# First cross attention of a decoder: one turn per loop body, written pairs of banks, weighed sums evicted by VectorE

## The reference

```python
NUM_HEADS, HEAD_DIM = 16, 16
SCALE = HEAD_DIM ** (-0.5)
Q = (x @ Wq.T).reshape(B, xN, NUM_HEADS, HEAD_DIM)
KV = (z @ Wkv.T).reshape(B, zN, 2, NUM_HEADS, HEAD_DIM)
K, V = KV[:, :, 0], KV[:, :, 1]
attn = jnp.einsum('bqhd,bkhd->bhqk', Q, K) * SCALE
attn = jax.nn.softmax(attn, axis=-1)
O = jnp.einsum('bhqk,bkhd->bqhd', attn, V).reshape(B, xN, DIM)
return O @ Wo.T
```

## Time and profile before

| What | Value |
|---|---|
| runs of the kernel, us | 3433.4, 3438.81, 3424.18; median 3433.4 |
| the profiled execution | 3433.98 us, its span 3432.2 us |
| mean granted TensorE clock | 0.972 |
| PE busy over the span | 3200.4 us (93%) |
| PEld / DVE / ACT / POOL busy | 2364.1 / 1767.5 / 1515.0 / 866.3 us |
| instructions recorded | 77662 |
| the changed stage, turn 0 to the start of turn 15 | 641.70 to 1169.72 us of the span |
| row maxima, L1779 | 256, mean 906 ns |
| exponents, L1726 | 256, mean 668 ns |
| packets of the queues of kind "instruction" | q8 123 with 2.02 MB, q14 29 with 0.24 MB |

### The profile page before, as it was taken

The page is one execution under the profiler, slowest core; times in us unless marked ns, Lnnn a source line. Parts: engine busy times, 40 slices in busy tenths (PEclk is TensorE's granted clock), DMA queues, the critical chain, the costliest instruction groups (busy, mean ns, idle before and its releaser), DMA issues. The chain is left out here.

```text
span 3432.2 us, 77662 instructions
## 1 busy us (share of the span) xinstructions
PE 3200.4 (93%) x26274; PEld 2364.1 (69%) x26275; DVE 1767.5 (51%) x4684; ACT 1515.0 (44%) x4278; POOL 866.3 (25%) x982
## 2 busy tenths in 40 slices
PE   8999999898988899999998999999999999999982
PEld 6777776455555566677776776777777777767871
DVE  4555555555555555222223654666666666663433
ACT  4555555344444421222222326666666666642220
POOL 1000000211111100233332110132323323346773
PEclk9999999899999999999999999999999999999996
DMA  8500000300000041211113000010000000025774
GB/s 276 164 0 0 0 0 0 145 13 11 14 13 13 30 147 51 66 32 30 30 26 79 17 0 5 25 40 19 17 13 11 14 13 12 25 75 151 210 207 133
DMA packets 136484, 182.54 MB, mean 53 GB/s; under 512 B 36156, under 2 KB 108601, under 8 KB 135308
## 3 DMA queue, kind: packets, MB, share of 16 engines
q1 hardware_dynamic: 84112, 133.96, 12.6%
q0 software_dynamic: 45760, 26.67, 4.8%
q10 hardware_dynamic: 6460, 19.66, 1.6%
HBM read 116.11 MB, written 103.61 MB: 64 GB/s over the span
## 5 line engine op out<-in xcount | busy, mean ns | idle before, releaser
L1309 DVE TENSOR_REDUCE e_nmx<-PS 128x1 f32<-128x361 f32 x416 | 221.3, 532 | 340.8 <-PE PS L1156 334.9
L931 POOL DMA_INDIRECT slot_rows<-r_row,r_rows_now x256 | 256.6, 1002 | 336.8 <-DVE e_p L1316 290.2
L1779 DVE TENSOR_REDUCE b_nmx<-PS 100x2 f32<-100x722 f32 x256 | 224.9, 906 | 216.8 <-PE PS L1571 216.8
L1156 PE MATMUL PS<-e_cT,e_qT 128*128 128x361 f32 x832 | 333.4, 483 | 0.0
L2709 PE MATMUL PS<-c_wgu,c_tile_xT 128*128 x912 | 290.7, 462 | 7.4 <-issue 6.6
L1261 ACT ACTIVATE e_pT<-PS 121x384 f32<-121x384 f32 (+1 forms) x416 | 199.0, 479 | 220.6 <-PE PS L1163 220.5
L1163 PEld LDWEIGHTS PS<-ident,e_p 128*121 128x121 f32 x1248 | 198.0, 184 | 96.2 <-ACT e_pT L1261 0.4
L1266 ACT ACTIVATE e_p<-PS,e_nmx 128x361 f32<-128x361 f32 x416 | 232.4, 559 | 36.2 <-DVE e_nmx L1309 36.2
L2709 PEld LDWEIGHTS PS<-c_wgu,c_tile_xT 128*128 128x128 f32 x912 | 169.8, 191 | 84.2 <-issue 9.4
L1156 PEld LDWEIGHTS PS<-e_cT,e_qT 128*128 128x128 f32 x832 | 145.9, 190 | 115.0 <-issue 108.6
L2973 POOL DMA_INDIRECT sum<-f_y,f_y_token x128 | 199.5, 1559 | 73.8 <-issue 46.9
(11 more groups left out here) (345 smaller groups left out, 6556.6 us busy)
## 6 DMA issues: line engine op xcount, KB each, us to landing
f_w<-in_f_W SPq DMA_DIRECT2D x64, 384.0 KB, 3.8
slot_rows<-a_empty SPq DMA_DIRECT2D x1, 21504.0 KB, 65.3
f_xg<-slot_rows SPq DMA_DIRECT2D x64, 336.0 KB, 4.0
c_wgu<-in_c_GU ACTq DMA_DIRECT2D x8, 1408.0 KB, 6.9
sum<-X SPq DMA_DIRECT2D x2, 3200.0 KB, 58.2
f_sums<-sum SPq DMA_DIRECT2D x16, 400.0 KB
b_cT<-in_ctx_T SPq DMA_DIRECT2D x32, 181.5 KB, 2.4
e_cT<-in_ctx_T SPq DMA_DIRECT2D x32, 181.5 KB, 2.3
```

What stands on the lines that cost most here:

```text
L931: pool.indirect_dma_start(out=self.rows, in_=self.row[:, u, :], in_offset=None, out_offset=bass.IndirectOffsetOnAxis(ap=self.rows_now[:, u ...
L1156: sr.fill_done(pe.matmul(sr.at(f"s{m}", ROWS, CTX), qT[:, at:at + ROWS], cT[:, u, 0:CTX], start=True, stop=True), f"s{m}")
L1309: dve.tensor_reduce(nmx[:, m:m + 1], sr.at(f"s{m}", ROWS, CTX), AX.X, ALU.max, negate=True).then_inc(max_ready, 1)
L1779: sr.move_done(dve.tensor_reduce(nmx[:, g // PAR % 2, 2 * half:2 * half + 2, 16 * (1 - r)], sr.both(f"s{g}{half}", S, CTX), AX.X, ALU.max, ...
```

## The change

It has three parts.

1. `qT` has one buffer. Before ScalarE overwrites it (in slot 1), VectorE copies the part that the shift of slot 2 still needs (the last tile of element 1) to a new tile `kept`, at the end of slot 0's shift; ScalarE waits for that on a new semaphore `queries_kept`. With one buffer the `par` argument goes away everywhere, and the loop body holds one turn: 15 passes, turns 0 to 14, and turn 15 written out.
2. `Pairs.plan` takes the pair of each name as a list. Slots 0 to 6 have the same pairs as before; in slot 7 the names take 1, 2, 1, 2 (7, 8, 7, 8 modulo 3) instead of 1, 2, 0, 1.
3. `move_sums` moves from ScalarE to VectorE. It stands at the end of a slot, ahead of the next slot's row maxima.

Besides, `parity_made` and `marks_made` become one semaphore.

```diff
-    def plan(self, names):
-        self.bank = {name: n % self.n for n, name in enumerate(names)}
-        self.order = {name: n // self.n for n, name in enumerate(names)}
-        self.per = [len(range(b, len(names), self.n)) for b in range(self.n)]
+    def plan(self, names, pairs):
+        self.bank = {name: pair % self.n for name, pair in zip(names, pairs)}
+        self.order = {name: sum(self.bank[m] == self.bank[name] for m in names[:n]) for n, name in enumerate(names)}
+        self.per = [sum(self.bank[m] == b for m in names) for b in range(self.n)]
...
-        qT = sb("qT", [128, 2, T, PAR, 2 * S])
+        qT = sb("qT", [128, T, PAR, 2 * S])
+        kept = sb("kept", [128, PAR, S])
...
         sr = Pairs(k, 0, 3).plan([f"{a}{group(n, by)}{half}" for n in range(GROUPS)
-                                  for a, by in (("s", SCORED), ("p", TURNED)) for half in range(2)])
+                                  for a, by in (("s", SCORED), ("p", TURNED)) for half in range(2)],
+                                 [n + x for n in range(GROUPS) for x in ((0, 1, 2, 3) if n < GROUPS - 1 else (0, 1, 0, 1))])
...
-                turn(-1, 1, False, True)
-                with pe.Fori(0, (TURNS - 1) // 2) as m:
-                    for par in range(2):
-                        turn(2 * m + par, par, True, True)
-                turn(TURNS - 2, 0, True, True)
-                turn(TURNS - 1, 1, True, False)
+                turn(-1, False, True)
+                with pe.Fori(0, TURNS - 1) as i:
+                    turn(i, True, True)
+                turn(TURNS - 1, True, False)
...
-                def move_queries(i, to):
+                def move_queries(i):
+                    if not isinstance(i, int) or i >= 0:
+                        act.wait_ge(queries_kept, i + 1)
                     mr.wait_full(act, "q", i)
...
-                        if ahead(n, WEIGHED, this, nxt):
-                            move_sums(n, i)
                         if not this:
                             load_ahead(n)
...
+                    of = kept if g == GROUPS - PAR else qT[:, tile, :, u * S:(u + 1) * S]
...
+                def move_sums(n, i):
+                    g = group(n, WEIGHED)
+                    mr.wait_full(dve, f"o{g}", i)
+                    mr.move_done(dve.tensor_copy(sums[:, g // G, g % G, :], mr.at(f"o{g}", 128, S)), f"o{g}")
...
                         if n % PAR == 0 and ahead(n, SHIFTED, this, nxt):
-                            shift(n, i, par)
+                            shift(n, i)
+                        if this and n == 0:
+                            dve.tensor_copy(kept[:], qT[:, T - 1, :, S:2 * S]).then_inc(queries_kept, 1)
                         if nxt and n == 1:
                             statistics(i + 2)
                         if nxt and n == 5:
                             mr.wait_full(dve, "xT", i)
                             apply(i + 2)
+                        if ahead(n, WEIGHED, this, nxt):
+                            move_sums(n, i)
```

More of the change, by code:

```diff
@@ L1557, in values, with scores @@
                     mr.fill_done(last, f"v{u}{c0}")
-                def scores(n, i, par):
+                def scores(n, i):
                     g = group(n, SCORED)
@@ L1571, in scores @@
                         last = pe.matmul(sr.one(f"s{g}{a // 2}", a % 2, S, CTX),
-                                         qT[rows, buffer(n, SCORED, par), tile, r, u * S:(u + 1) * S],
+                                         qT[rows, tile, r, u * S:(u + 1) * S],
                                          kT[rows, u, tile, 0:CTX], start=True, stop=True)
@@ L1657, in piece, with turn @@
                         out(int(m[1]), i)
-                def turn(i, par, this, nxt):
+                def turn(i, this, nxt):
                     for n in range(GROUPS):
                         if ahead(n, SCORED, this, nxt):
-                            scores(n, i, par)
+                            scores(n, i)
                         elif not this:
@@ L1713, in move_values @@
                     mr.move_done(last, f"v{u}{c0}")
-                def move_queries(i, to):
+                def move_queries(i):
+                    if not isinstance(i, int) or i >= 0:
+                        act.wait_ge(queries_kept, i + 1)
                     mr.wait_full(act, "q", i)
                     for r in range(PAR):
-                        last = act.activation(qT[:, to, :, r, :], mr.at("q", 128, T, 2 * S), ACT.Copy,
+                        last = act.activation(qT[:, :, r, :], mr.at("q", 128, T, 2 * S), ACT.Copy,
                                               scale=parity[:, r:r + 1])
@@ L1727, in exponents, with piece @@
                                                     sr.both(f"p{g}{half}", KEYS, CH * S), ACT.Exp), f"p{g}{half}")
[L1729 to L1733, removed]
+                def piece(m, i):
                     if m == "xT":
@@ L1736, in piece @@
                     elif m == "q":
-                        move_queries(i, 1 - par)
+                        move_queries(i)
                     elif m[0] == "k":
@@ L1748, in turn @@
                             if this if m in OWN else nxt:
-                                piece(m, i, par)
+                                piece(m, i)
                         if ahead(n, TURNED, this, nxt):
                             exponents(n, i)
-                        if ahead(n, WEIGHED, this, nxt):
-                            move_sums(n, i)
                         if not this:
                             load_ahead(n)
-                act.wait_ge(parity_made, 1)
+                act.wait_ge(marks_made, 1 + PAR)
                 act.wait_ge(prepared, PREPARED)
[L1759 to L1764, removed]
+                turn(-1, False, True)
+                with act.Fori(0, TURNS - 1) as i:
+                    turn(i, True, True)
+                turn(TURNS - 1, True, False)
             @block.vector
@@ L1781, in maxima, with shift @@
                                  f"s{g}{half}")
-                def shift(n, i, par):
+                def shift(n, i):
                     g = group(n, SHIFTED)
                     u, tile = g // G, g % G // PAR
+                    of = kept if g == GROUPS - PAR else qT[:, tile, :, u * S:(u + 1) * S]
                     mr.wait_full(dve, f"w{g}", i)
@@ L1849, in _ @@
                                       AX.X, ALU.add).then_inc(marks_made, 1)
-                dve.wait_ge(marks_made, 2)
+                dve.wait_ge(marks_made, 1 + PAR)
                 dve.tensor_scalar(unmarked[:], mark[:], -1.0, 1.0, ALU.mult, ALU.add).then_inc(marks_made, 1)
                 dve.wait_ge(prepared, PREPARED)
[L1853 to L1858, removed]
+                turn(-1, False, True)
+                with dve.Fori(0, TURNS - 1) as i:
+                    turn(i, True, True)
+                turn(TURNS - 1, True, False)
         sr.done(TURNS)
```

12 lines of the change are left out of this document (5 added, 7 removed).

## The result

The changed kernel takes 3385.9 us (median of 4 runs, 3385.3 to 3387.2), the kernel before 3436.1 over the runs beside it (3424.2 to 3444.7); the ratio is 0.9857 with an interval of 0.9826 to 0.9888. The forecast was 3387.

The account below looks back on a forecast made before the run. TensorE bounds the first cross attention, its two-turn code fetched anew in each pass. 37.0 + 0.5 + 9.0 = 46.5 us off the profiled 3434.0 gives 3387 us, range 3378 to 3400; forecast 70%.

Parts of the forecast that it names:

- One turn per pass: First cross attention, TensorE's loop: code of one turn is kept, so six jumps at 6.17 us each go; 37.0 us gain.
- At most 0.3 each: Bound on the cost of the 14 new jumps in TensorE's loop, taken at 0; 4 us at most.
- the 6.17 us: Predicted price of each of the six old jumps: longer gap 2.8, second gap 1.1, the rest from half the clock.
- Written pairs: Slot 7 to next slot 0: scores wait for only the first exponent, 0.56 us less at 16 starts; 9.0 us gain.
- comes on top: At the six jumps the written pairs' gain adds to the 37.0, reckoned down to a turn still having the 0.76.
- Sums on VectorE: Copies of weighed sums, about 0.26 us each (bound 0.42), lie under the scores' matmuls on TensorE; cost 0.
- The kept copy: VectorE's 128x200 copy once a turn after slot 0's shift fits before its next maximum, even beside GpSimd; cost 0.
- 37.0 + 0.5 + 15 x 0.56: Stage terms: jumps gone 37.0 us, turn 14 becoming a pass of the loop 0.5, written pairs 0.56 a start.
- Rival A: TensorE's one-turn body isn't kept either, each of 14 jumps costs 6.17 us: 39.9 us slower, 3474; 4%.
- B: Rival: branch and register work replace the second exponent's wait, turn starts still cost 0.76; 9.0 us less gain, 3396; 11%.
- C: Rival: VectorE becomes late with the row maxima in slots 7 and 5, 1 us a turn, 16 us: 3403; 9%.
- D: Rival: TensorE's body is kept only in part, a jump costs about half (3 us): 3430, no difference; 3%.

Follow-up runs that it names:

- shifted kernel: Changed kernel with two turns per body on TensorE alone, plus twelve more small matmuls ahead of the stage's loop (20 instead of 8); 3420.7 us.
- Part 1 alone: Changed kernel with the old order of pairs and the weighed sums back on ScalarE after the exponents; one turn per body and kept copy stay; 3403.3 us.

## Why the prediction was right, step by step

- **One turn per pass, 37.0 us.** Right in mechanism and sum. The code is fetched once, the branches are short, and with TensorE alone back at two turns all of the gain is gone. With the old pairs, so with this step but not the next, fourteen turns take 14 x 32.72 = 458.1 us where turns 0 to 13 took 494.80: 36.7. "At most 0.3 each" for the new jumps was not needed: a gap of 0.10 leaves no room for them. What I didn't see is that the 6.17 us is no constant: 4.5 to 8.5 in seven kernels and two stages, and where the loop lies in the code is one reason. A forecast for the opposite change would have missed by 10 us.
- **Written pairs, 0.56 at 16 starts, 9.0 us.** 0.57 by the turns (32.72 and 32.15). The gap itself shrank by more, from 0.76 to 0.10, and one more wait of 0.19 in the turn (three where there were two) gave part of it back. But the claim that this "comes on top" at the six jumps holds only since the jumps went too: alone, Part 2 brought nothing, though by my sum it would have had ten uncovered starts. At the jumps it met longer branches, with the read ahead 0.1 to 0.2 us before them instead of 0.4 to 0.9. Since the shifted kernel, also with written pairs and two turns per body, has a pass of 69.63 us against 71.39 before, this loss seems to hang on where the code lies. So in a body that doesn't stay, the worth of Part 2 can't be read off its wait; that it is always nothing there isn't shown.
- **Sums on VectorE, 0.** Right: the copy took 262 ns as estimated, and with the sums on ScalarE nothing changes.
- **The kept copy, 0.** Right, and the meeting with GpSimd can be seen. In the changed kernel the copy took 253 ns in most turns and 467 in the first (over my bound of 0.42), and in 14 turns the GpSimd instruction beside it (L1509) took 0.85 us instead of 0.66; so GpSimd is busy 6.07 us in a turn instead of 5.88. In the kernel of Part 1 alone it is the other way round: the copy took over 550 ns in 15 of 16 turns, and GpSimd's instruction kept its 0.66. First the changed kernel, then two rows of Part 1 alone:

```profile
L1509 POOL TENSOR_SCALAR b_kM<-b_kT,b_unmarked,b_mark x128: 653/659/854, 607.6 to 1119.0; 128x363 f32<-128x363 f32 x128
...
L1835 DVE COPY b_kept<-b_qT x16: 253/556/559, 650.1 to 1141.0; 128x200 f32<-128x200 f32 x16
...
L1509 POOL TENSOR_SCALAR b_kM<-b_kT,b_unmarked,b_mark x128: 657/659/667, 611.6 to 1131.8; 128x363 f32<-128x363 f32 x128
```

  The Trainium skill ("SBUF — State Buffer", "Who interferes with whom") has it that the two exclude each other; the trace agrees, in that one of the two is longer each time. It cost the path nothing.
- **The rest.** Turns 0 to 14 lasted 528.02 us and now 1124.76 - 642.29 = 482.47: 45.6 less, against 37.0 + 0.5 + 15 x 0.56 = 45.9 by my steps. Draining took 0.7 longer, with a mean clock of 0.87 instead of 1.00. The forecast against the profiled execution was 46.5, and 48.7 was measured; the difference lies outside this stage. Of the 44.3 us at the end of this stage 41.9 were left at the first product of the last stage, which then gave 6.9. That the median came out within about 1 us of 3387 is therefore in part luck. From its first to its last matmul the last stage took 301.9 to 302.5 us in the five profiled kernels whose body in the changed stage didn't stay, and 292.7 to 300.3 in the nine others, with the same code of its own in all. So some 2 to 10 us of the total go together with the change by a way that no run here shows; this stays open. It is too small to make the gain doubtful and too large to read single parts from totals.
- **Rival A** was the Trainium skill's rule of two 16 KB lines ("Runtime: NRT & Kernel Launch", "Instruction fetch mechanics"). It fails for TensorE: bodies up to 1320 matmuls and loads stay. The same section gives TensorE a memory of 2048 instructions; 1656, or 1749 with the register work that I count in the trace, did not stay. The 16 KB packets and the wait at a far jump are as it says. B, C and D did not occur.

## What to carry to other kernels

Look for packets of kind "instruction" inside a loop, and for turns of the same work that differ by some us with a lower granted clock: both were here the signs of a body too long for its engine. If so, shorten the body first (here a copy of 253 ns replaced a second buffer), and only then remove small waits, since a jump that waits for code can take their gain back. And read such parts from the turns' rows, not from totals.

## What the runs showed of the hardware

- TensorE's loop bodies of 1008, 1104 and 1320 matmuls and loads were fetched once; those of 1656, 2016 and more in each pass. Branches take 0.21 us in the first case and 3.3 to 4.5 in the second (medians 3.4 to 4.2).
- Moving a loop by some 48 instructions made each branch 0.8 us and each pass 3.2 us shorter, 16 us over the kernel. At 28 jumps the target's packet took 1.4 to 2.0 us where a read ahead began within 0.2 us of the branch, and 0.9 to 1.3 where it began earlier.
- A stall of 3.5 us on TensorE was followed by 6.7 us at 1.2 GHz, which cost another 2.25 us: TensorE was busy 33.04 instead of 30.79 us in that turn.
- A copy of 128x200 on VectorE and a GpSimd instruction that met in SBUF lengthened one another in turn: either GpSimd's took 0.85 us instead of 0.66, or the copy 0.55 instead of 0.25.
